# TensorE's side work in one batch behind every fourth slot of a fused attention kernel

## What is computed

```python
# layer 2: additive attention, then a mixture of experts
Wi = einsum('bnd,ed->bne', ln(t), W)
scores = einsum('d,bijd->bij', v, tanh(Wi[:, None] + Wi[:, :, None]))   # 784 x 784 tanh vectors of 128
t = t + einsum('bij,bjd->bid', softmax(scores), ln(t))
t = t + top2_experts(ln(t))                                           # 8 experts, 128x128 each
# layer 3: linear attention, then a spectral transform
t = t + linear_attention(ln(t))                                       # elu(q)+1, elu(k)+1, causal
t = t + spectral(ln(t))      # 16 filters, plus and minus, convolved over the tokens, each times a 128x128 matrix
```

## Time and profile before

| what | value |
|---|---|
| median of 3 runs (lowest, highest) | 12586.33 us (12584.73, 12590.29) |
| the profiled execution: its time, its span | 12589.56 us, 12587.8 us |
| PE, DVE, ACT busy over the span | 94%, 91%, 87% |
| first two layers | until about 6180 us |
| passes 0 and 1 (up to 6867.5 us) | 347.0 and 340.5 us |
| passes 2 to 15 (6867.5 to 12226.6 us) | 5359.1 us, 382.8 us each |
| the tail | 361.2 us |

### The profile page before, as it was taken

One profiled execution on the slowest core, in us unless ns is written; L12 is line 12 of the kernel. 1 busy time (PEld: TensorE's weight loads), 2 busy tenths in 40 slices (PEclk: granted clock), 3 DMA queues, 4 the chain that ended last, 5 costly groups with the idle time before them and its releaser, 6 DMA issues. The chain is left out here.

```text
span 12587.8 us, 298131 instructions
## 1 busy us (share of the span) xinstructions
PE 11857.0 (94%) x123040; PEld 5799.6 (46%) x123040; DVE 11395.9 (91%) x21555; ACT 10922.3 (87%) x7444; POOL 128.1 (1%) x103
## 2 busy tenths in 40 slices
PE   8999999999999999999767999999999999999999
PEld 3333333333333333333223555555555555555556
DVE  9999999999999999999899888889888898888881
ACT  8999999999999999999788888888888888888872
POOL 0000000000000000000000000000000000000000
PEclk9999999999999999999889999999999999999999
DMA  0000000000000000000110111111111111111113
GB/s 14 2 7 2 4 4 2 7 2 4 4 2 7 2 4 4 2 4 2 30 37 10 50 48 51 54 51 53 47 49 52 53 51 49 49 51 53 50 56 106
DMA packets 290040, 355.08 MB, mean 28 GB/s; under 512 B 28040, under 2 KB 242960, under 8 KB 288656
## 3 DMA queue, kind: packets, MB, share of 16 engines
q1 hardware_dynamic: 288656, 335.48, 9.1%
HBM read 314.14 MB, written 21.23 MB: 27 GB/s over the span
## 5 line engine op out<-in xcount | busy, mean ns | idle before, releaser
L276 ACT ACTIVATE c_ring<-c_xn,c_w_neg 128x1568 f32<-128x1568 f32 x3824 | 5791.7, 1604 | 282.2 <-PE c_acc L235 275.6
L235 PE MATMUL c_acc<-c_ring,c_onehot 128*32 128x392 f32 x68608 | 5764.6, 493 | 139.2 <-DVE c_ring L434 79.9
L1084 ACT ACTIVATE t_ring<-t_ring 128x3120 f32<-128x3120 f32 (+56 forms) x2160 | 4518.5, 2113 | 679.9 <-DVE t_ring L1406 667.2
L426 DVE TENSOR_SCALAR c_ring<-c_xn,c_w 128x1568 f32<-128x1568 f32 x4752 | 4573.5, 1036 | 95.5 <-PE c_acc L235 95.5
L1406 DVE TENSOR_SCALAR t_ring<-t_proj 128x784 f32<-128x784 f32 (+63 forms) x10240 | 3935.0, 457 | 573.4 <-PE t_psS L990 561.1
L235 PEld LDWEIGHTS c_acc<-c_ring,c_onehot 128*32 128x32 f32 x68608 | 2216.4, 110 | 3661.3 <-issue 3213.5
L990 PE MATMUL t_psS<-t_ring,t_vhot 128*32 128x392 f32 (+15 forms) x36864 | 2478.5, 402 | 154.7 <-ACT t_ring L1084 136.8
L947 PE MATMUL t_psC<-t_filter_work 128*128 128x392 f32 (+3 forms) x6144 | 1639.2, 401 | 8.1 <-ACT t_filter_work L1071 8.0
L990 PEld LDWEIGHTS t_psS<-t_ring,t_vhot 128*32 128x32 f32 x36864 | 1001.2, 111 | 1029.6 <-issue 367.9
L947 PEld LDWEIGHTS t_psC<-t_filter_work 128*128 128x128 f32 x6144 | 1133.2, 192 | 652.3 <-issue 32.9
L434 DVE SCALAR_TENSOR_TENSOR c_ring<-c_xn,c_w,c_ring 128x784 f32<-128x784 f32 x1280 | 1267.8, 1034 | 95.8 <-ACT c_ring L276 94.3
(11 more groups left out here) (227 smaller groups left out, 3405.2 us busy)
## 6 DMA issues: line engine op xcount, KB each, us to landing
t_filter_work<-in_toep_dram SPq DMA_DIRECT2D x256, 393.0 KB, 3.4
t_filter_work<-mix_scratch SPq DMA_DIRECT2D x512, 192.0 KB, 2.4
t_filter_work<-in_toep_dram SPq DMA_DIRECT2D x256, 197.0 KB, 2.6
t_filter_work<-mix_scratch SPq DMA_DIRECT2D x512, 64.0 KB, 1.8
mix_scratch<-t_filter_work SPq DMA_DIRECT2D x4, 2048.0 KB, 9.5
c_xin<-in_x_dram SPq DMA_DIRECT2D x8, 784.0 KB, 4.3
x_scratch<-c_x1o SPq DMA_DIRECT2D x8, 784.0 KB, 3.4
t_proj<-x_scratch SPq DMA_DIRECT2D x16, 392.0 KB, 3.5
```

The lines of the kernel that those rows point to most:

```text
L235: mm = pe.matmul(acc[32 * g:32 * g + 32, ch, 0:HALF], onehot[:, 31 - r:63 - r], ring[:, s % RING, g, ch * HALF:(ch + 1) * HALF], start=(s ...
L276: ins = act.activation(tile4(ring[:, s % RING, g, :]), window(xn, tap), ACT.Relu, bias=w0_neg[:, tap, 4 * r + g:4 * r + g + 1])
L426: dve.tensor_scalar(tile4(ring[:, s % RING, g, :]), window(xn, tap), w0[:, tap, 4 * r + g:4 * r + g + 1], 0.0, ALU.subtract, ALU.max).then ...
L1084: act.activation(ring[:, st % RINGS, 0:n], ring[:, st % RINGS, 0:n], ACT.Tanh).then_inc(th.s, 1)
```

## The change

PE calls `step` no longer after every slot but after slots 3, 7, 11, ..., 131, 134 (`BATCHES`, 34 a pass), and everything due by then runs in one batch. `batch(B, rank)` names the slot of batch B plus a rank within it: first `conv(2B)` (FIRST, 0.0), then pieces of the other chains (EARLY, 0.1), two `mixin` (MIX, 0.3), more pieces (LATE, 0.5), and `conv(2B+1)` last (SECOND, 0.8). `in_step` now takes the pieces in the order of their due values instead of track by track. All tables are new, also those that DVE and ACT read. The order of the tail comes from the same tables. The transposes that fill softmax blocks 2 to 5 now go to the PSUM bank `psB` in one piece each, with events of their own (`pF`, `eF`), instead of to `psF`; `rowmax` and what follows is split into pieces accordingly. The arithmetic and the number of matmuls are the same.

```diff
+GROUP = 4
+BATCHES = {min(GROUP * B + GROUP - 1, NS - 1) for B in range((NS + GROUP - 1) // GROUP)}
+def batch(B, rank):
+    return min(GROUP * B + GROUP - 1, NS - 1) + rank
+FIRST, EARLY, MIX, LATE, SECOND = 0.0, 0.1, 0.3, 0.5, 0.8
...
-AT_MOE = dict(logits=44, bias_add=45, exp=46, rank=47, rank2=48, gate=49, turn=50, evac=51, bias=52, bias_used=53, y=54)
-AT_LIN = dict(q=77, zq=78, eq=79, qout=80, k=79, zk=80, ek=81, kout=82, v=81, vout=82, a=83, n=98)
-AT_STU = dict(u=124, uev=126, res=14, resev=16, conv=1, mix=7, ar=[5, 71], out=[70, 1])
+AT_LN = [dict(stats=28, aggr=30, norm=32, turn=batch(8, EARLY), evac=35), dict(stats=80, aggr=82, norm=84, turn=batch(21, EARLY), evac=87),
+         dict(stats=117, aggr=118, norm=120, turn=batch(30, EARLY), evac=123)]
...
+AT_STU = dict(u=batch(31, EARLY), uev=127, res=batch(3, LATE), resev=16, conv=[batch(u // 2, (FIRST, SECOND)[u % 2]) for u in range(64)], conved=[4 * (u // 2) + (3, 5)[u % 2] for u in range(64)],
+              mix=[batch(1 + m // 2, MIX) for m in range(64)], ar=[batch(1, EARLY), batch(17, EARLY)], out=[68, 1])
...
         def in_step(slot, due, tracks):
-            for n, track in enumerate(tracks):
-                while due[n] is not None and due[n] <= slot:
-                    due[n] = next(track, None)
+            while True:
+                n = min((n for n in range(len(tracks)) if due[n] is not None and due[n] <= slot), key=lambda n: due[n], default=None)
+                if n is None: break
+                due[n] = next(tracks[n], None)
...
         def alone(step):
-            for slot in range(NS): step(slot)
+            for slot in range(NS): step(slot + 0.99)
...
+                    W(pe, eF, blk - 2, d)
+                    transposes(lambda t: S[:, blk, 128 * t:128 * t + 128], lambda t: psB[:, 128 * (t - blk):128 * (t - blk) + 128], pF.s, range(blk, NT))
...
-                        step(st)
+                        if st in BATCHES: step(st + 0.99)
```

More of the change, by code:

```diff
@@ L528 @@
 OLD_USES = USE["out6"]; NEXT_USES = 6
-AT_EVAC = 1
[L532 to L535, removed]
@@ new lines, in batch @@
+def batch(B, rank):
+    return min(GROUP * B + GROUP - 1, NS - 1) + rank
+FIRST, EARLY, MIX, LATE, SECOND = 0.0, 0.1, 0.3, 0.5, 0.8
+AT_EVAC = 1
+AT_OLD = {2: dict(fill=batch(0, EARLY), filled=3, rowmax=3, diag=3, m=batch(1, EARLY), sub=7, exp=8, out=batch(2, EARLY), add=11),
+          3: dict(fill=batch(0, LATE), filled=4, rowmax=6, diag=10, m=batch(2, LATE), sub=12, exp=13, out=batch(3, EARLY), add=15),
+          4: dict(fill=batch(1, EARLY), filled=7, rowmax=11, diag=14, m=batch(3, LATE), sub=16, exp=17, out=batch(4, EARLY), add=19),
+          5: dict(fill=batch(1, LATE), filled=8, rowmax=15, diag=18, m=batch(4, LATE), sub=20, exp=21, out=batch(5, EARLY), add=23),
+          6: dict(rowmax=17, diag=22, m=batch(5, LATE), sub=24, exp=25, out=batch(6, EARLY), add=27)}
@@ new lines @@
+AT_NEW = {0: dict(fill=[batch(9, EARLY), batch(9, LATE)], filled=[39, 40], rowmax=41, diag=41, m=batch(10, EARLY), sub=43, exp=44, out=batch(11, EARLY), add=47),
+          1: dict(fill=[batch(20, LATE), batch(21, EARLY)], filled=[84, 87], rowmax=88, diag=88, m=batch(22, EARLY), sub=91, exp=92, out=batch(23, EARLY), add=95)}
+AT_LN = [dict(stats=28, aggr=30, norm=32, turn=batch(8, EARLY), evac=35), dict(stats=80, aggr=82, norm=84, turn=batch(21, EARLY), evac=87),
+         dict(stats=117, aggr=118, norm=120, turn=batch(30, EARLY), evac=123)]
@@ new lines @@
+AT_MOE = dict(logits=batch(9, EARLY), bias_add=39, exp=40, rank=41, rank2=42, gate=43, turn=batch(11, EARLY), evac=47, bias=batch(12, EARLY), bias_used=51,
+              y=[batch(13 + i // 2, (EARLY, LATE)[i % 2]) for i in range(14)], added=[4 * (13 + i // 2) + 3 + i % 2 for i in range(14)])
+AT_LIN = dict(q=batch(22, EARLY), zq=91, eq=92, qout=93, k=batch(22, LATE), zk=92, ek=93, kout=94, v=batch(23, EARLY), vout=95,
+              a=[batch(24 + i // 4, (EARLY, EARLY, LATE, LATE)[i % 4]) for i in (0, 2, 4, 6, 7, 8, 9)], apart=[99, 100, 103, 104, 104, 107, 107],
+              n=[batch(27 + t // 4, (EARLY, EARLY, LATE, LATE)[t % 4]) for t in range(7)], npart=[111, 111, 112, 112, 115, 115, 116])
@@ L765, in one_pass @@
                 if not no(b, 0):
-                    for k in range(3): root(lnv, lns, k + 1, b - 1)
+                    for k in range(2): root(lnv, lns, k + 1, b - 1)
                 if not no(b, NI - 1): root(lnv0, lns0, 1, b + 1)
+                if not no(b, 0): root(lnv, lns, 3, b - 1)
             def last():
@@ L907, in after @@
                     ins.then_inc(pN.s, 1)
-                yield AT_LN[2] + LN_AT["turn"]
+                yield AT_LN[2]["turn"]
                 ln(2)
+            last_old = lambda d: NI - 1 if isinstance(d, int) and d == NI - 1 else d + 1
             def turn_u(d):
@@ L963, in spectral @@
                 for u in range(4 * NK):
-                    todo += [(AT_STU["conv"] + 2 * u, 3, conv, (u,)), (AT_STU["mix"] + 2 * u, 2, mixin, (u,))]
+                    todo += [(AT_STU["conv"][u], 3, conv, (u,)), (AT_STU["mix"][u], 2, mixin, (u,))]
                 for at, _, part, args in sorted(todo, key=lambda x: x[:2]):
@@ L1063, in spectral @@
                 for u in range(4 * NK):
-                    at = AT_STU["conv"] + 2 * u + 1
-                    if at - 2 < AT_STU["resev"] <= at:
+                    at = AT_STU["conved"][u]
+                    if u and AT_STU["conved"][u - 1] < AT_STU["resev"] <= at:
                         yield AT_STU["resev"]
@@ L1254, in ln @@
                 dve.tensor_scalar(var[:, :], mv[:, :, 1], LN_EPS, None, ALU.add).then_inc(ready.s, 1)
-                yield at + LN_AT["norm"]
+                yield at["norm"]
                 W(dve, rooted, k, d)
@@ L1315, in after @@
                 for i in range(14):
-                    yield AT_MOE["y"] + i + 1
+                    yield AT_MOE["added"][i]
                     t, h = i // 2, i % 2
```

115 lines of the change are left out of this document (54 added, 61 removed).

## The result

| | median of 4 runs (lowest, highest) | ratio, 95% interval |
|---|---|---|
| before | 12586.2 us (12584.73, 12590.29) | |
| the change | 12864.38 us (12862.33, 12871.08) | 1.0222 (1.021 to 1.0234) |

The change is 2.2% slower. The forecast of 12498 us was wrong, in its sign as well, and its range (to 12665) did not hold the time.

What follows compares the result with a forecast made beforehand. It took PE to bound most of the 14 full passes, with ACT or DVE limiting some stages. From 12589.6 us, -137 for the passes and +46 for the tail gave 12498 us, range 12390 to 12665.

Steps and rivals of the forecast that it cites:

- It fits with 1.5 us to spare. I price it at nothing: Waits inside a pass: a 10.9 us loop fits a 12.4 us group of four slots, so they add 0.
- The lap: First stage: DVE's fill 2 us, two tanhs 5.4, copy 0.5, wide `conv` 1.6, a slot of scores 1.4; 10.9 in all.
- The condition that the prediction names: Loop of a batch: it does not fit if DVE has over 1.5 us of side work between the two fills.
- passes 0 and 1: The first two passes, limited by DVE: change of 0, give or take 3 us each.
- the tail: Neighbouring `conv` wait for ACT's copy, 62 x 0.81 = 50 us, less 4: +46, from 361 to 407 us.
- The limits by stage: Full pass: no stage falls below its busiest engine; stages sum to 373.0 us against 383.0, about 9.8 off the mean pass.
- a loss: Slots 96-127: PE 67.1 and DVE 67.7 us of work alternate as limits, so 77.5 us, now 75.4.
- What a batch costs PE: Full pass: 0.35 us a batch, 65 batches fewer, so PE's work shrinks by 22.8 us a pass.
- the estimate in the prediction: Cost of a batch by the skill's rule: two drains of some 128 cycles, 0.11 us, 7 us a pass.
- DVE's waits for PE: Full pass: down from 39.5 to about 25 us.
- Rival D: Within batches: PE waits for ACT's copy, 17 us a pass; passes of 390, 12737 us in all; chance 0.2.
- What would show it: Signs against the forecast: PE waiting for L1094's copy, stage 96-127 well above 77.5, clock below 0.97, tail of 361.

Runs made afterwards that it cites:

- experiment 1: The change with both of ACT's copies of `conv` one tanh earlier, behind slots 4B+5 and 4B+7: 12551.26 us, ratio 0.9974.
- fours: The kernel before with PE's due pieces run behind every fourth slot alone, DVE's and ACT's tables untouched: 12591.72 us, ratio 1.0004.
- Pairs: The kernel before with PE's due pieces run behind every second slot alone, DVE's and ACT's tables untouched: 12530.76 us, ratio 0.9956.
- threes: The kernel before with PE's due pieces run behind every third slot alone (45 batches): 12431.11 us, ratio 0.9876.
- experiment 8: The change with eight unread matmuls of 64 columns ahead of the wait of `conv(2B+1)` in eight batches: 12867.0 us, ratio 1.0224.
- experiment 6: The kernel before, unbatched, with each of ACT's copies of `conv` one tanh later: 12722.42 us, ratio 1.0109.
- experiment 5: The change with both of ACT's copies of `conv` two tanhs earlier, behind slots 4B+4 and 4B+6: 12614.24 us, ratio 1.0024.
- experiment 12: The kernel before with PE's pieces behind every second slot and ACT's copies of `conv` one tanh earlier: 12538.36 us, ratio 0.9961.

## Why the prediction was wrong

**The failed step** is "It fits with 1.5 us to spare. I price it at nothing". The lap that it adds up has 10.9 us of fills, tanhs, copy, `conv` and scores, against 12.4 of a group. I added the lap up for the first stage, where a group takes 12.4 us, and took it for all. In the first stage it held: PE waits 2.1 us for the copy there in pass 8 of the change, and 27.2 in the other stages. In slots 32 to 79 the forecast itself left a group only 10.75 us. The tanhs are shorter there (1.7 us for 2.7), but the lap shown has 13.2 us: 2.1 for the fill of slot 37, 1.8 for its tanh, 1.6 in which the next tanh waits for DVE's fill (1.3 of it DVE's evacuation of scores), 1.6 for that tanh, 0.8 for ACT's own evacuation, 0.5 for the copy, 3.3 for `conv` and 1.5 of scores. The waiting, ACT's evacuation and the fallen clock I had not counted. The condition that the prediction names, over 1.5 us of DVE's side work between the fills, isn't what failed in this lap: 1.3 us were enough. And the wide `conv` was read too short, at 1.6 us: it takes 2.0 until the next matmul starts (9256.84 to 9258.84 in experiment 1), so the spare was 1.1 us even in the first stage. A second lap over the stage with the tightest group would have shown it before. Last, I looked at the gate at the end of a batch alone, not at the one at its start.

Moving the two copies by one tanh, and nothing else, gives 22.2 us a pass back, 14 x 22.2 = 311 of the 364 us between 12498 and 12862. That part is shown. Of the other 53, some 48 are passes of 376.4 where the forecast had 373.0, 9 are passes 0 and 1, and the tail is 3 below its forecast. With the late copies gone, the rest of the forecast can be held against experiment 1, pass 8, cut at the same slots:

| stage | before | forecast | the change | copies one earlier |
|---|---|---|---|---|
| slots 0-31 | 103.2 | 99 | 102.6 | 99.1 |
| slots 32-79 | 136.8 | 129 | 140.3 | 129.2 |
| slots 80-95 | 54.7 | 54 | 55.9 | 55.7 |
| slots 96-127 | 75.4 | 77.5 | 84.0 | 79.5 |
| the last seven | 12.9 | 13.5 | 15.0 | 12.3 |
| sum | 383.0 | 373.0 | 397.8 | 375.8 |

- **The limits by stage** come out within some 2 us each (the last column's cuts are good to some 0.7 us), but that is partly luck. In slots 32 to 79 of experiment 1 PE is busy 125.9 us, as forecast (126.1); fours on the old tables have 129.9 there, so batches alone bring 5.3 us of the forecast 9.1. The rest goes with the new tables. In slots 96 to 127 PE is busy 76.2 us where the forecast had 67.1 and fours on the old tables have 68.4: the forecast moved DVE's work between the stages and forgot PE's (the products of the linear attention, L919, are 20 matmuls in this stage, and 4 in those fours). So this stage does lose by the new tables (79.5, and 73.7 in fours with the old ones), as "a loss" had it, but twice as much.
- **What a batch costs PE** was over-sized. The pass less PE's idle time is 362.8 us before, 358.4 in the change and 351.4 in experiment 1. Of the forecast 22.8 us that is 11.4, 0.18 us for each of 65 batches; if PE's time at half clock is counted at the full one, it is 14.7, 0.23 each, in the change as in experiment 1. Pairs, threes and fours give 0.22 to 0.26 counted so. The gap to 0.35 isn't explained by any run here. The drains that the Trainium skill names ("TensorEngine Tiling (Array Packing)", Key Properties) would make 0.11 us by the estimate in the prediction; no run here shows a batch as cheap as that.
- **The tail** was right in size, +43.0 against +46, and in its cause: 63 waits between neighbours, 0.71 us each, against 62 of 0.81. What the experiments give back is less, 18.0 us by alternating and 33.8 with the copies moved as well. Of the 9.2 us that stay, 3.7 are PE's busy time and 5.5 its idle time, in which 5.0 of waits for `t_side` and 4.4 for the copy are the longest.
- **Passes 0 and 1** lose 8.9 us together where I had 0, give or take 3 each. They have no `conv`. The granted clock fell (0.87 from 0.91 in pass 1). The new tables aren't needed for this: fours on the tables of before lose more, pass 1 takes 12.1 us more than before:

```profile
6527.70:6880.30 352.60, 248.32 (x2687) 120.61 (x2687) 334.97 (x931) 290.74 (x158) 7.13 (x4) 0.85 0.01 2
```

In pass 1 pairs lose 2.2 us and threes 4.1, so the loss comes with the grouping itself. DVE, the limit there, is busy as before (334.97 us, 334.50), but waits for PE: 1.8 us in pass 1 of the kernel before, 9.8 in the change (7.3 of them for its scores) and 13.3 in fours (11.6 for side results).

- **DVE's waits for PE** were to fall to about 25 us. They fell to 33.8 in pass 8 of the change and to 21.8 in that of experiment 1.
- **Rival D** had the mechanism and a price of 17 us a pass. It came to 22 from both gates, and most of that in slots 32 to 79 and 96 to 127 instead of the first stage (11.1 and 4.5 us of the table, 3.5 in the first). In slots 80 to 95, where DVE is the limit, PE's waits for the copy (9.1 us in the change) cost under 1 us. Its chance of 0.2 was far too small, since its one argument against was the spare.
- **What would show it** did: PE waits for L1094's copy within batches, the stage 96-127 is above 77.5, and the clock is 0.96.

What stays open is why threes win by so much over pairs and fours. PE's relief is nearly that of fours (352.2 us of work a pass against 351.6) and its idle time that of the unbatched kernel. The missing wait for `t_S` in slots 0-31 speaks for the way in which the due slots of before happen to fall into threes, but no run here moves them, so the group's length isn't ruled out.

## What to carry to other kernels

Before work of one in-order engine is gathered into batches, list for both ends of a batch which result it needs and how many items of the other engine's program stand ahead of that result; then add up the lap for the group with the most side work on the filling engine, not for the mean group. If two waits stand in one row, removing one can show little of what removing both does (8.2 or 5.8 of 22.2 us here), so an experiment with one alone says little. A coarser schedule is best tried first on the old tables, with every small group size: here a few lines gave 1.2%, and the full rewrite cost 2.2%.

## What the hardware showed

- Idleness of TensorE brings its granted clock down, and work behind the waits pays for it: 2.17 us became 3.41 behind 2.55 us of idleness. Between the change and experiment 1 this is 7.0 of the 22.2 us of a pass. But keeping the clock up is no cure for a wait: with unread matmuls, 13.9 us less at half clock brought 2.3 us of a pass net in experiment 8, and in experiment 6 the kernel lost 1.1% with less time at half clock than before.
- An evacuation that an in-order engine runs one tanh (2.1 us) later costs 9.6 us a pass with 64 of them, even without batches (experiment 6). One tanh too early cost 4.3 us a pass between experiments 1 and 5, where PE then waited for tanhs (16.4 us a pass), and nothing that can be told in pairs (experiment 12), where it did not.
